# Third attention of a four-layer block: row normalisation moved from VectorE to ScalarE, its bias made on GpSimd, mask additions in half as many matmuls

## What is computed

```python
def _layernorm(x, axis=-1, eps=1e-05):
    m = jnp.mean(x, axis=axis, keepdims=True)
    v = jnp.var(x, axis=axis, keepdims=True)
    return (x - m) / jnp.sqrt(v + eps)

# third attention: 16 heads of 8 columns
scores = jnp.einsum('bhqd,bhkd->bhqk', q, k) / jnp.sqrt(jnp.float32(dk))
scores = jnp.where(masks[:, None, :, :], scores, jnp.float32(-1000000000.0))
attn = jax.nn.softmax(scores, axis=-1)
out = jnp.einsum('bhqk,bhkd->bhqd', attn, v)
...
# third feed-forward: 8 experts, the two best by router logits
logits_BSE = jnp.einsum('BSD,DE->BSE', x, router_kernel_DE)
weights_BSK, indices_BSK = jax.lax.top_k(probs_BSE, TOP_K)

x = x + jnp.tanh(g_xattn[2]) * _L2_xattn_ref(_layernorm(x, axis=-1), ctx_1024, ctx_1024, mask, ...)
x = x + jnp.tanh(g_ffn[2]) * _L2_ffn_ref(_layernorm(x, axis=-1), ...)
```

## Time and profile before

| | us |
|---|---|
| runs | 2526.29, 2531.04, 2535.46 |
| median | 2531.04 |
| the profiled execution's own time | 2529.54 |
| its span in the profile | 2527.8 |
| the third attention in it | about 1376 to 1784 |

### The profile page before, as it was taken

The page is one execution under the profiler, slowest core; times in us unless marked ns, Lnnn a source line. Parts: engine busy times, 40 slices in busy tenths (PEclk is TensorE's granted clock), DMA queues, the critical chain, the costliest instruction groups (busy, mean ns, idle before and its releaser), DMA issues. The chain is left out here.

```text
span 2527.8 us, 80307 instructions
## 1 busy us (share of the span) xinstructions
PE 2166.0 (86%) x33256; PEld 1672.9 (66%) x33267; DVE 1790.4 (71%) x5057; ACT 1356.3 (54%) x2507; POOL 1176.6 (47%) x1728
## 2 busy tenths in 40 slices
PE   6999999999996969998555899996699958898597
PEld 5887878877774746776444677774466637777375
DVE  3777777777773648888895689887455559988354
ACT  3555555555552327876997555551122159888132
POOL 1334343434344541114775135556466666885444
PEclk8999999999997979999777899996799969988599
DMA  7330000000005621110000011111555422332363
GB/s 194 108 122 28 25 27 24 24 21 20 19 18 164 186 72 53 54 56 13 1 1 11 28 41 54 52 50 40 157 162 157 126 71 79 109 98 71 99 185 103
DMA packets 213963, 184.63 MB, mean 73 GB/s; under 512 B 33420, under 2 KB 189654, under 8 KB 213600
## 3 DMA queue, kind: packets, MB, share of 16 engines
q1 hardware_dynamic: 194144, 142.52, 19.2%
q0 software_dynamic: 19456, 36.99, 4.3%
HBM read 102.01 MB, written 72.68 MB: 69 GB/s over the span
## 5 line engine op out<-in xcount | busy, mean ns | idle before, releaser
L614 POOL DMA_INDIRECT slots<-row,put x256 | 258.7, 1010 | 208.3 <-issue 127.6
L1945 PE MATMUL experts_H<-experts_xs_t,experts_w 128*128 128x512 f32 x576 | 266.8, 607 | 6.7 <-DMA experts_b<-in_F_b 2.6
L1099 ACT ACTIVATE l_prob_t<-l_banks 128x512 f32<-128x512 f32 x256 | 132.2, 602 | 144.1 <-PE l_banks L1216 113.5
L1471 POOL TENSOR_TENSOR l_var_eps<-l_mv,eps 128x1 f32<-128x1 f32 x64 | 12.3, 191 | 412.5 <-DVE l_mv L1552 412.5
L1963 PE MATMUL experts_Y<-experts_w,experts_hid 128*128 128x128 f32 x1664 | 197.8, 275 | 3.5 <-DVE experts_y L1893 2.6
L1810 POOL DMA_INDIRECT rows<-experts_y,experts_idx x160 | 155.7, 973 | 92.4 <-DVE experts_y L1889 51.9
L1274 PE MATMUL l_banks<-l_val,l_prob_t 128*64 128x18 f32 x5120 | 198.6, 213 | 0.0
L1963 PEld LDWEIGHTS experts_Y<-experts_w,experts_hid 128*128 128x128 f32 x1664 | 191.7, 192 | 5.4 <-issue 5.4
L1274 PEld LDWEIGHTS l_banks<-l_val,l_prob_t 128*64 128x64 f32 x5120 | 187.1, 141 | 8.0 <-issue 0.5
L1507 DVE TENSOR_REDUCE l_top<-l_S 128x16 f32<-128x1024 f32 x64 | 78.3, 1224 | 160.8 <-PE l_S L1650 160.8
L1945 PEld LDWEIGHTS experts_H<-experts_xs_t,experts_w 128*128 128x128 f32 x576 | 106.5, 195 | 116.4 <-issue 107.9
(11 more groups left out here) (312 smaller groups left out, 5954.3 us busy)
## 6 DMA issues: line engine op xcount, KB each, us to landing
experts_w<-in_F_w SPq DMA_DIRECT2D x104, 256.0 KB, 3.0
l_ctx_t<-in_ctx_t SPq DMA_DIRECT2D x96, 128.0 KB, 2.4
early_q_m<-l_q_t SPq DMA_DIRECT2D x384, 32.0 KB, 1.8
experts_xs<-slots SPq DMA_DIRECT2D x40, 264.0 KB, 3.0
slots<-l_empty SPq DMA_DIRECT2D x16, 536.0 KB, 4.0
experts_xs<-slots SPq DMA_DIRECT2D x16, 536.0 KB, 4.5
slots<-l_empty SPq DMA_DIRECT2D x16, 520.0 KB, 5.9
experts_xs<-slots SPq DMA_DIRECT2D x16, 520.0 KB, 4.8
```

The costliest lines, as they stand in the source:

```text
L614: pool.indirect_dma_start(self.slots, bass.IndirectOffsetOnAxis(ap=g.put[c][:, tile:tile + 1], axis=0), g.row[:, tile, self.sent_cols], No ...
L1099: nc.scalar.activation(prob_t[:, t.par(PROB), r, :], Z[:, r, :], ACT.Exp).then_inc(prob_done, 1)
L1945: nc.tensor.matmul(H[:, c, :], w1_s[:, t.par(2), c, :], xs_t[:, t.par(2), :], start=True, stop=True).then_inc(h_filled[c], 1)
```

## The change

Four edits, all in force in `l2` alone:

1. DVE no longer normalises rows for the attention (L988) and for the router (L756). ACT does it, at the end of its step, as `Identity(scale * x + bias)` with the reciprocal root as scale and a bias per row: two activations for the attention, two for the router.
2. POOL makes that bias, minus mean times reciprocal root: two more small operations for the attention and two for the router in each step, behind the power of both, each second one waiting for the first.
3. Waits: POOL's power waits for `xn_done` of two items before, DVE's BN_AGGR waits for `shift_done` of the item whose place it overwrites, ACT waits for `shift_done`.
4. The masks are added by one matmul of 512 columns for each bank, where there were two of 256.

```diff
+        self.by_scalar = kind == "top2"
@@ root, in POOL's step
             wait(pool, self.eps, t.done(s))
+            if self.by_scalar:
+                wait(pool, self.xn_done, t.done(s + 2))
@@
+    def shift_rows(self, nc, pool, t, s):
+        if t.live(s):
+            wait(pool, self.rstd_done, t.done(s))
+            nc.gpsimd.tensor_tensor(self.shift[:, t.par(s), :], self.mv[:, t.par(s), :, 0], self.rstd[:, t.par(s), :], ALU.mult).then_inc(
+                self.shift_part, 1)
+            wait(pool, self.shift_part, t.done(s))
+            nc.gpsimd.tensor_scalar(self.shift[:, t.par(s), :], self.shift[:, t.par(s), :], -1.0, None, ALU.mult).then_inc(self.shift_done, 1)
+
+    def normalise(self, nc, act, t, s):
+        if t.live(s):
+            wait(act, self.shift_done, t.done(s))
+            for tile in range(self.tiles):
+                last = nc.scalar.activation(self.g.xn[:, t.item(s) * self.tiles + tile, :], self.g.x[:, t.item(s) * self.tiles + tile, :], ACT.Identity,
+                                            bias=self.shift[:, t.par(s), tile:tile + 1], scale=self.rstd[:, t.par(s), tile:tile + 1])
+            last.then_inc(self.xn_done, 1)
@@ Router.dve
             wait(dve, self.part, n0)
+            if self.by_scalar:
+                wait(dve, self.shift_done, t.done(s + 2))
@@
-        if t.live(s + 1):
+        if t.live(s + 1) and not self.by_scalar:
             wait(dve, self.rstd_done, n1)
@@ POOL's step
+                if folded and t.live(NORM):
+
+                    wait(pool, rstd_done, t.done(NORM))
+                    nc.gpsimd.tensor_tensor(shift[:, t.par(NORM), :], mv[:, t.par(NORM), :, 0], rstd[:, t.par(NORM), :], ALU.mult).then_inc(shift_part, 1)
+                    wait(pool, shift_part, t.done(NORM))
+                    nc.gpsimd.tensor_scalar(shift[:, t.par(NORM), :], shift[:, t.par(NORM), :], -1.0, None, ALU.mult).then_inc(shift_done, 1)
+                if folded:
+                    tail.shift_rows(nc, pool, t, T0 + 1)
@@ DVE's step
-                if t.live(NORM) and not stable:
+                if t.live(NORM) and not stable and not folded:
                     normalise(t)
@@ ACT's step, at its end
+                if folded and t.live(NORM):
+
+                    wait(act, shift_done, t.done(NORM))
+                    wait(act, xv_filled, beats(t.t - 1, TURN, XV_BEATS))
+                    for tile in range(2):
+                        last = nc.scalar.activation(xn[:, t.par(NORM), tile, :], g.x[:, t.item(NORM) * 2 + tile, :], ACT.Identity,
+                                                    bias=shift[:, t.par(NORM), tile:tile + 1], scale=rstd[:, t.par(NORM), tile:tile + 1])
+                    last.then_inc(xn_done, 1)
+                if folded:
+                    tail.normalise(nc, act, t, T0 + 1)
@@ PE's step
-                    for tile in range(2):
-                        for r in range(4):
-                            last = nc.tensor.matmul(Z[:, r, 256 * tile:256 * tile + 256], g.const_bf[:, C_IDENT:C_IDENT + P],
-                                                    hide[:, 1, 2 * t.item(PROB) + tile, :].unsqueeze(1).broadcast_to([P, 4, 64]),
-                                                    start=False, stop=tile == 1)
+                    masks = hide[:, 1, 2 * t.item(PROB):2 * t.item(PROB) + 2, :]
+                    for r in range(4):
+                        last = nc.tensor.matmul(Z[:, r, :], g.const_bf[:, C_IDENT:C_IDENT + P], masks.unsqueeze(2).broadcast_to([P, 2, 4, 64]),
+                                                start=False, stop=True)
```

More of the change, by code:

```diff
@@ L560, in __init__ @@
         self.slots_clear = None
+        self.by_scalar = kind == "top2"
+        if self.by_scalar:
+            self.shift = ph.sb("tail_shift", [P, 2, tiles])
+            self.shift_part, self.shift_done = ph.sems("tail_shift_part tail_shift_done")
         self.loads = 16 * (1 + (bias is not None))
@@ L977, in statistics @@
                     wait(dve, stats_part, t.done(STAT))
+                    if folded:
+                        wait(dve, shift_done, t.done(STAT + 2))
                     for tile in range(2):
@@ L1213, in step @@
                 if folded and t.live(PROB):
-                    for tile in range(2):
-                        for r in range(4):
-                            last = nc.tensor.matmul(Z[:, r, 256 * tile:256 * tile + 256], g.const_bf[:, C_IDENT:C_IDENT + P],
-                                                    hide[:, 1, 2 * t.item(PROB) + tile, :].unsqueeze(1).broadcast_to([P, 4, 64]),
-                                                    start=False, stop=tile == 1)
+                    masks = hide[:, 1, 2 * t.item(PROB):2 * t.item(PROB) + 2, :]
+                    for r in range(4):
+                        last = nc.tensor.matmul(Z[:, r, :], g.const_bf[:, C_IDENT:C_IDENT + P], masks.unsqueeze(2).broadcast_to([P, 2, 4, 64]),
+                                                start=False, stop=True)
                     last.then_inc(p_filled, 1)
                 if folded and t.live(SCORE):
-                    for tile in range(2):
-                        for r in range(4):
-                            last = nc.tensor.matmul(X[:, r, 256 * tile:256 * tile + 256], g.const_bf[:, C_IDENT:C_IDENT + P],
-                                                    hide[:, 0, 2 * t.item(SCORE) + tile, :].unsqueeze(1).broadcast_to([P, 4, 64]),
-                                                    start=False, stop=tile == 1)
+                    masks = hide[:, 0, 2 * t.item(SCORE):2 * t.item(SCORE) + 2, :]
+                    for r in range(4):
+                        last = nc.tensor.matmul(X[:, r, :], g.const_bf[:, C_IDENT:C_IDENT + P], masks.unsqueeze(2).broadcast_to([P, 2, 4, 64]),
+                                                start=False, stop=True)
                     last.then_inc(s_filled, 1)
```

5 lines of the change are left out of this document (added).

## The result

| | before | changed |
|---|---|---|
| median of 20 runs each | 2530.49 us | 2539.08 us |
| the profiled execution's own time | 2529.54 us | 2544.15 us |
| its span | 2527.8 us | 2542.4 us |

The medians are 8.6 us apart. The ratio, by which every run here is judged, is 1.0025, 95% interval 1.0013 to 1.0037: 6.3 us slower (3.3 to 9.4), by less than the 0.3% that the prediction counted as a difference. The forecast of 2529, with 2520 to 2537, was too low.

The account below looks back on a forecast made before the run. PE with a short serial piece through DVE was taken to set full steps, DVE a share of every second one. 2529.5 - 3.5 - 1.0 + 1.1 + 1.65 = 2527.8 us, 2529.3 by the median; forecast 2529, range 2520 to 2537.

Parts of the forecast that it names:

- Full steps, -3.5 us: Third attention's full steps: relieving DVE shortens only the ten steps behind the router's choice of experts, 3.5 us in all.
- step behind a choice: Full step whose maxima follow the router's choice of experts, where DVE is late; forecast from 10.83 to 10.47 us.
- Masks, -1.0 us: Mask matmuls on PE: four fewer save 0.02 us in each of 64 groups, taken as 1.0 us.
- the rival built on it: Mask groups: 512 columns cost what 256 do, saving 14 to 29 us, about 2510 us; chance 0.05.
- ScalarE and GpSimd hidden in full steps, 0: Full steps: ACT's new activations and POOL's new bias operations fit ahead of the next exponentials, costing 0.
- First steps, 0 with half a microsecond either way: Phase start: first normalised rows come 0.85 us later, DVE's memsets sooner by as much; counted 0.
- Last exponentials late by their own engine, +1.1 us: Near the phase's end: the router's activations precede the last exponentials on ACT, delaying them and later scatters; +1.1 us.
- the bound of 1.6 us: Phase's end: most that could be lost if the wait let PE's clock fall one step sooner.
- The collision on ACT itself: Phase's end: the router's two activations stand ahead of the last exponentials in ACT's order; +1.1 us.
- Three pairs at the end, +1.65 us: Last scatters on POOL: three powers each followed by a bias pair of 0.55 us, +1.65 us.
- Sum: Whole kernel: all terms added to the profiled 2529.5 us give 2527.8 us, or 2529.3 by the median.

Follow-up runs that it names:

- e3: Kernel before with only the normalisation moved to ACT and its bias to POOL, masks as before; 2533.3 us, ratio 1.0005.
- e11: The kernel before, unchanged, traced once more; one run, 2534.6 us.
- e1: The changed kernel, run again unaltered; 2537.4 us, ratio 1.0034.
- e4: Changed kernel, but from the router's item 24 (step 34) VectorE normalises the router's rows and GpSimd makes no router bias; 2528.7 us, ratio 0.9984.
- e5: Changed kernel plus eight unused 256-column matmuls in steps 37 and 38 where PE waits for the exponentials; 2530.4 us, ratio 0.9996.
- e8: Changed kernel, but VectorE normalises and GpSimd makes no bias for the router's last 4 items alone (steps 38 on); 2532.9 us, ratio 1.0002.
- e6: e4 with GpSimd's bias pair kept to the end, its result unused, VectorE waiting for it and normalising; 2530.2 us, ratio 0.9999.
- e13: e4 run again unaltered; 2532.4 us, ratio 1.0001.
- e2: Kernel before with only the masks changed to one 512-column matmul for each bank; 2532.4 us, ratio 0.9988.
- e18: e14 run again unaltered; one run, 2518.2 us.
- e7: Changed kernel, but for the router's last 8 items VectorE makes the bias and ScalarE still normalises; 2539.8 us, ratio 1.0039.
- e10: e4 plus two unused 128-column ScalarE copies in each step from 34 on; 2531.6 us, ratio 0.9999.
- e14: e4 plus two unused 128-column ScalarE copies in steps 34 and 35 alone; 2532.3 us, ratio 0.9996.

## Why the prediction was wrong

*Full steps, -3.5 us*: right. The step behind a choice went from 10.83 to 10.46 (forecast 10.47). e3 gives -3.6 us against the profiled kernel before; against e11, which had more short falls of the clock among its full steps, -5.5.

*Masks, -1.0 us*: the group came as forecast, 0.87 us, or 0.217 a matmul of 512 columns. The Trainium skill's 131 ns a matmul ("TensorE: Matmul & The Clock Gate", Back-to-back issue gap) doesn't show here; the rival built on it is out. The step kept 0.2 to 0.4 us of the forecast 1.0 (e3 against the changed kernel).

*ScalarE and GpSimd hidden in full steps, 0*: right. ACT waited 1.84 us for PE ahead of L1137 in the row above. The activation is 0.48 to 0.49 us, near the 0.5 taken; by the Trainium skill ("ScalarE: Activation LUTs", What ACT_TABLE_LOAD costs) it was 0.48, and the trace agrees.

*First steps, 0 with half a microsecond either way*: right. From DVE's first statistics of the phase to the first scores it is 9.7 us in all sixteen traces with the new normalisation and 9.4 in the four without, 0.3 more.

*Last exponentials late by their own engine, +1.1 us*: **this is the step that failed.** The prediction had PE at 2.4 GHz up to the last exponentials and ACT's activations as what makes them late. In the changed kernel the exponentials of steps 37 and 38 waited 2.96 and 2.65 us for PE, at 1.2 GHz, and not for the activations. The prediction had put PE's clock into half a sentence, as a loss of at most 1.6 us if the clock fell one step sooner. It fell two steps sooner, in step 36, and again in step 37, and the scatter of step 39 came 6.8 us later. For the bound of 1.6 us the prediction gives no working, and it rests on one trace of one kernel in which the clock held through step 37. The collision on ACT itself is hidden and not refuted. In e1, whose clock held to 13 us, the step 37 exponentials were not late (10.2 us), but in step 38 the activations were over at 1722.62, 19.6 us after the last scores:

```profile
1721.74 0.88 ACT L647 ACTIVATE row<-row,l_tail_shift,l_tail_rstd 128x128 f32<-128x128 f32 x2 [0.31 <-POOL l_tail_shift L641]
```

In e4, whose clock held, these exponentials start at 18.4. By my estimate from these two traces the order on ACT would have cost 1.2 us, near the forecast 1.1, had PE kept its clock; as it fell, PE was later still (22.2 us).

That the clock is not steady in the kernel before either, e11 shows: it can have a fall 8 us after the last scores too, but a single short one, which costs 0.8 us at step 39. What makes it one short fall there and a long or repeated one in the changed kernel's three traces is known only in part. e5 speaks for a share of PE's wait of 1.18 us in the second fall; e1 and e8 against e4, e6 and e13, at the same dip, for a share of ScalarE's activations or of VectorE's earliness. Going back to VectorE at the end took away the loss, by the times and in both traces (e4, e13), GpSimd's 3.0 us surely, the early fall as far as a dip of 148 shows it. Why the clock falls so early stays open.

*Three pairs at the end, +1.65 us*: the mechanism was right and the size too small. Measured 2.4 between the two profiles, and 3.0 for the pairs themselves (1.95, 1.90 and 1.90 us from power to scatter, 0.92, 0.91 and 0.92 before); over all traces the stretch is 47.3 to 48.0 us with the pair and 44.3 to 44.9 without. The pair is 0.55 to 0.6 as taken; the term left out that the indirect DMA behind it starts 0.55 to 0.59 us after POOL's last instruction and not 0.19.

*Sum*: +0.3 - 4.0 + 6.8 + 2.4 = +5.5 us in the phase, where the forecast had -1.75, against 6.3 us (3.3 to 9.4) measured. The two profiled spans are 14.6 us apart. The rest is outside the phase: the changed kernel's starts 4.25 us later (DVE's first statistics at 1380.14 and 1375.89; 1374.0 and 1382.9 in its two other traces), and behind its last scatter come 4.8 us more. The three traces of the changed kernel take 749 to 751 us there. Sixteen of the others take 740 to 749, e2 takes 754. No instruction of the change runs there. The granted clock goes with this time, as a mean over the whole stretch: 0.88 in the changed kernel's profile, e1 and e2 (751, 751 and 754 us), 0.89 before (747), 0.91 in e18 (740). No single place makes the difference: over the 40 us that begin 280 us after the last scatter it is 0.83 in the changed kernel and 0.90 before, but 0.83 in e7 and e10 too, which take 746 and 742. Whether the change has a share in this stays open.

## What to carry to other kernels

Work moved off an engine that is late only in every second step gives back that step's wait and nothing more; its price is looked for at the phase's ends, where the covers of the full steps are gone. There the old assignment can be kept: e4 switches back for the last eight items, and neither of its two traces shows the losses. And a bound on what the clock can do, taken from one trace, is a guess: two traces of the kernel before show its first fall at 8 and at 23 us.

## What the runs showed of the hardware

- POOL's indirect DMA starts 0.19 us after a power (0.72 us long) that was issued ahead of it, but 0.50 to 0.60 us after a dependent pair of 128x2 operations, in every trace that has the pair between the last scatters.
- TensorE's granted clock fell to 1.2 GHz right behind stretches in which it was busy 5.68 of 6.00 us (the changed kernel, no wait over 0.35 us in it), and held at 2.4 GHz through 4.67 of 6.00 (before). Two executions with the same PE rows to 0.02 us over the 25 us up to the last scores and 6.4 us beyond (e10, e14) were then granted different clocks.
- ScalarE's copies of 128 constant columns take 0.50 us for two, and two activations of 128 columns with pointers for scale and bias 0.87 to 0.88 us.
